# Layer 2's message table as three bf16 parts gathered by TensorE alone, and four lane places in layers 1 and 3

## The reference

```
layer 0: out = [x, mean over src of edge_attr, u]; three times relu(out @ W.T + b), batch norm
layer 1: relu((sum of x[src] by dst / count + x) @ W.T + b)
layer 2: message = [x[src], x[dst]] @ Wmsg[type] + bmsg[type]; agg = mean by dst
         h = [x, agg] @ Wupd + bupd; x + gelu(layer norm(h))
layer 3: sum by dst of dinv[src] * w * dinv[dst] * (x[src] @ W), self loops; relu, batch norm
```

## Time and profile before

| | |
|---|---|
| median of 3 runs | 3917.97 us (3916.83 to 3924.28) |
| profiled execution | 3916.97 us, of which the span of the trace is 3915.2 us |
| busy share of the span | PE 74%, PEld 65%, DVE 60%, ACT 35%, POOL 48% |
| TensorE's granted clock, mean over the span | 0.96 |

### The profile page before, as it was taken

One profiled execution on the slowest core, in us unless ns is written; L12 is line 12 of the kernel. 1 busy time (PEld: TensorE's weight loads), 2 busy tenths in 40 slices (PEclk: granted clock), 3 DMA queues, 4 the chain that ended last, 5 costly groups with the idle time before them and its releaser, 6 DMA issues.

```text
span 3915.2 us, 90566 instructions
## 1 busy us (share of the span) xinstructions
PE 2906.6 (74%) x22101; PEld 2552.1 (65%) x22102; DVE 2356.3 (60%) x6762; ACT 1381.0 (35%) x4186; POOL 1888.7 (48%) x1870
## 2 busy tenths in 40 slices
PE   7455444444459976776998899999879967777996
PEld 6233322222258855776997599999868957776995
DVE  7666666666658885333777544444446774344777
ACT  0111000000024444554664231221246337887534
POOL 4777777777730034776000177777732006774000
PEclk9999999999999988998998999999989978998998
DMA  6444444444458815776884344444467816786883
GB/s 216 147 144 144 145 145 142 142 143 143 141 190 271 271 40 185 267 272 218 288 285 137 131 161 159 155 164 163 122 180 225 272 58 237 267 275 203 276 285 119
DMA packets 430910, 736.77 MB, mean 188 GB/s; under 512 B 71488, under 2 KB 207305, under 8 KB 429820
## 3 DMA queue, kind: packets, MB, share of 16 engines
q1 hardware_dynamic: 336876, 498.35, 41.2%
q0 software_dynamic: 93968, 237.72, 16.6%
HBM read 486.89 MB, written 294.72 MB: 200 GB/s over the span
## 4 chain that ended last, share of the span: by engine, by line
POOL 30%; PE 26%; issue 19%; DMA 13%; DVE 5%; ACT 3%; SPq 2%; DVEq 1%; POOLq 1%; ACTq 0%
POOL slots L704 19%; PE ps L1324 17%; DMA gbuf<-ring_raw,to_blk 7%; POOL gbuf L752 7%; POOL ring_raw L757 3%; DMA ring_raw<-gbuf 3%; DMA ring_raw<-msg_rows,tables 2%; PE ps L1200 2%; PE ps L1367 1%; PE ps L1404 1%; PE ps L1395 1%; ACT ring_raw L942 1%; PE ps L1476 1%; PE ps L1460 1%; DVE stats L1813 1%
## 5 line engine op out<-in xcount | busy, mean ns | idle before, releaser
L752 POOL DMA_INDIRECT gbuf<-ring_raw,to_blk x731 | 752.3, 1029 | 737.4 <-ACT ring_raw L945 383.3
L704 POOL DMA_INDIRECT slots<-ring_raw,idx_edges x782 | 764.3, 977 | 241.6 <-issue 241.6
L1324 PE MATMUL ps<-ring_raw,hot_raw 128*128 128x128 f32 (+2 forms) x6576 | 797.5, 280 | 108.9 <-DVE hot_raw L1749 47.5
L1324 PEld LDWEIGHTS ps<-ring_raw,hot_raw 128*128 128x128 f32 x6576 | 769.6, 194 | 144.4 <-issue 78.9
L1749 DVE TENSOR_TENSOR hot_raw<-dst_lane,lane_ids 128x512 f32<-128x512 f32 x903 | 626.2, 694 | 70.0 <-ACT dst_lane L906 48.8
L1356 PE MATMUL ps<-big,hot_raw 128*128 x5160 | 584.9, 276 | 22.9 <-ACT ring_raw L945 18.5
L1356 PEld LDWEIGHTS ps<-big,hot_raw 128*128 128x128 f32 x5160 | 579.1, 192 | 29.2 <-issue 28.9
L1235 PE MATMUL ps<-big 128*49 128x343 bf16 (+6 forms) x784 | 263.5, 489 | 397.0 <-DVE big L1645 395.7
L945 ACT COPY ring_raw<-ps 128x512 f32<-128x512 f32 x473 | 277.5, 588 | 647.2 <-DMA gbuf<-ring_raw,to_blk 429.0
L1759 DVE TENSOR_TENSOR big<-big,ps 128x128 f32 (+2 forms) x1032 | 293.6, 284 | 314.6 <-PE ps L1324 311.2
L1235 PEld LDWEIGHTS ps<-big 128*49 128x49 bf16 x784 | 113.9, 159 | 539.6 <-DVE big L1645 305.5
(11 more groups left out here) (264 smaller groups left out, 3919.6 us busy)
## 6 DMA issues: line engine op xcount, KB each, us to landing
ring_raw<-gbuf SPq DMA_DIRECT2D x669, 268.0 KB, 3.5
ring_raw<-in_edge_attr SPq DMA_DIRECT2D x111, 448.0 KB, 3.8
zr<-lane_rows SPq DMA_DIRECT2D x129, 384.0 KB
ring_raw<-slots SPq DMA_DIRECT2D x153, 272.0 KB, 3.4
zt<-lane_rows SPq DMA_DIRECT2D x86, 384.0 KB
big<-slots SPq DMA_DIRECT2D x105, 272.0 KB, 3.2
big<-gbuf SPq DMA_DIRECT2D x105, 268.0 KB, 3.8
pays_raw<-key_rows SPq DMA_DIRECT2D x112, 224.0 KB
```

The source lines that it names most:

```text
L704: pool.indirect_dma_start(edges, bass.IndirectOffsetOnAxis(idx_edges[0:n, u, j:j + 1], 0), edge_rows[0:n, u, j, :], None).then_inc(scatter ...
L752: pool.indirect_dma_start(gbuf, bass.IndirectOffsetOnAxis(to_blk[:, t:t + 1], 0), node_rows[:, r, :], None, bounds_check=NBLK - 1, oob_is_ ...
L1324: ins = pe.matmul(bank(r % 3, width), hots[:, r, j * P:(j + 1) * P], rows[:, j, 0:width], start=j == 0, stop=j == BLK - 1)
```

## The change

- The table `msgs` is now three bf16 tables: high, middle and low part, whose sum is the float32 value. ScalarE copies the high part from PSUM, VectorE writes the rest into a ring of five (`rests`), ScalarE copies the middle part from it, GpSimd subtracts to the low part. The bias is added in PSUM by a second matmul with 3 rows, whose bf16 parts GpSimd prepares behind layer 1's scatters (`split_bias`).
- All six tiles of a round are gathered by TensorE, by bf16 one-hots, with 9 matmuls for each edge position. `msg_rows`, its writes, the fetches and the scatters of fetched rows are gone.
- In layers 1 and 3 the lanes of odd rounds have two places of their own (`lane_odd`, in `B`), so a load may run a round ahead. Edge weights are copied (`keep_weights`) to a table of their own, as the parts take the memory of `pays_raw`.

```
-MIX = RING
-WIDE = MIX - 1
-SPAN = {1: RING, 2: WIDE, 3: RING}
-GATHERED = {1: 0, 2: TILES, 3: TILES + RR * WIDE}
+PARTS = 3
+RESTS = 5
+GATHERED = {1: 0, 2: TILES, 3: 2 * TILES}
...
+        msgs = memory[:, 0:PARTS * PART // 2].bitcast(BF16).rearrange("p (s e) -> p s e", s=PARTS)
...
-        hots3 = hot_raw[:, :].rearrange("p (s t n) -> p s t n", s=2, t=TYPES)
+        hots3 = hot_raw[:, TYPED:HOTS].bitcast(BF16).rearrange("p (s t n) -> p s t n", s=2, t=TYPES)
...
+            def load_turn_lanes(layer, h, odd, free=True):
+                i = h * 2 + odd
                 for r in range(0, RING, LANE_SETS):
+                    if free:
+                        sp.wait_ge(src_hots, i * RING + (GATHERED[layer] - 2 * RING + r + LANE_SETS))
...
-                        sp.wait_ge(st["g2"]["r"], NEAR + (i + 1) * STEP)
-                        sp.dma_start(table[:, i * STEP:(i + 1) * STEP, :],
-                                     msgs[:, i * STEP:(i + 1) * STEP, :]).then_inc(msgs_out, 16)
...
-                    for i in range(RR):
-                        for r in range(WIDE):
-                            scatter_block(i, r)
-                            if r == 0 and i > 0:
-                                scatter_fetched(i - 1)
-                            if r == WIDE - 2 and i > 0:
-                                pool.wait_ge(fetched_sent, 16 * i)
-                                pool.sem_inc(issued, 1)
-                            if r >= WIDE - 2:
-                                for k in range(2):
-                                    fetch_messages(i, 2 * (r - WIDE + 2) + k)
-                    scatter_fetched(RR - 1)
+                for i in range(RR):
+                    for r in range(RING):
+                        scatter_block(i, r)
+            def low_parts(n):
+                pool.wait_ge(mid_ready, n + 1)
+                pool.tensor_tensor(part_of(2, n), rests[:, n % RESTS, :], part_of(1, n), ALU.subtract).then_inc(low_ready, 1)
...
             scatter_blocks(1)
+            keep_weights()
+            split_bias()
+            for n in range(GROUPS):
+                low_parts(n)
             scatter_blocks(2)
...
+            def high_part(n):
+                act.wait_ge(st["g2"]["m"], n + 1)
+                act.copy(part_of(0, n), bank(6 + n % 2, TYPES * D)).then_inc(high_ready, 1)
+            def mid_part(n):
+                act.wait_ge(st["g2"]["r"], n + 1)
+                act.copy(part_of(1, n), rests[:, n % RESTS, :]).then_inc(mid_ready, 1)
+            def parts(i, last=False):
+                for n in range(i * STEP, (i + 1) * STEP):
+                    high_part(n)
+                    if n:
+                        mid_part(n - 1)
...
             g2_operands(3)
             g2_copy(3)
             g2_operands(4)
+            parts(3)
             ln_sqrt(2, 2)
             g2_copy(4)
             g2_operands(5)
+            parts(4)
...
+                    for r in range(RING):
+                        pe.wait_ge(src_hots, i * RING + (base + r + 1))
+                        pe.wait_ge(staged, i * RING + (base + r + 1))
                         for j in range(BLK):
                             for t in range(TYPES):
-                                ins = pe.matmul(bank(r)[:, j * P:(j + 1) * P], hots3[:, (odd + r) % 2, t, j * P:(j + 1) * P],
-                                                msgs_flat[:, bass.ds(at[r] + t * D, D)],
-                                                start=t == 0, stop=t == TYPES - 1)
+                                for k in range(PARTS):
+                                    ins = pe.matmul(bank(r)[:, j * P:(j + 1) * P], hots3[:, r % 2, t, j * P:(j + 1) * P],
+                                                    msgs[:, k, bass.ds(at[r] + t * D, D)],
+                                                    start=t == k == 0, stop=t == TYPES - 1 and k == PARTS - 1)
...
+                    n = i * STEP + j
+                    if n > 1:
+                        pe.wait_ge(st["g2"]["r"], n - 1)
+                    pe.matmul(bank(6 + n % 2, TYPES * D), zt2[:, j, :],
                               wcat[:, 0:TYPES, :].rearrange("p k d -> p (k d)"),
-                              start=True, stop=True).then_inc(st["g2"]["m"], 1)
+                              start=True, stop=False, skip_group_check=True)
+                    pe.matmul(bank(6 + n % 2, TYPES * D), part_ones, bias_parts, start=False, stop=True,
+                              skip_group_check=True).then_inc(st["g2"]["m"], 1)
...
-            pe.wait_ge(st["g2"]["r"], NEAR + GROUPS)
+            pe.wait_ge(low_ready, GROUPS)
             gather(2)
...
             def g2_results(i, js=range(STEP)):
                 for j in js:
+                    n = i * STEP + j
+                    dve.wait_ge(high_ready, n + 1)
+                    if n >= RESTS:
+                        dve.wait_ge(low_ready, n - RESTS + 1)
+                    dve.tensor_tensor(rests[:, n % RESTS, :], bank(6 + n % 2, TYPES * D), part_of(0, n),
+                                      ALU.subtract).then_inc(st["g2"]["r"], 1)
```

More of the change, by code:

```diff
@@ L96, in fills_before, with of @@
 def fills_before(stage, r):
-    return sum(EVEN if s in (("g", 0), ("g", 1)) else RR for s in FILLS[:FILLS.index(stage)] if s[0] == "g" or r % LANE_SETS == 0)
+    def of(s):
+        if s[0] == "g":
+            return EVEN if s[1] < 2 else RR
+        if s[1] == 2:
+            return RR if r % LANE_SETS == 0 else 0
+        return (EVEN, ODD, 0)[r % LANE_SETS]
+    return sum(of(s) for s in FILLS[:FILLS.index(stage)])
 LCOLS = 86
@@ L319, in gnn_kernel @@
         to_blk = sb("to_blk", [P, TILES], U32)
-        lanes = sb("lanes", [P, TILES * BLK], BF16)
-        lanes_t = sb("lanes_t", [P, TILES * BLK], BF16)
+        edge_w = sb("edge_w", [P, TILES * BLK])
+        lanes, lanes_t = (edge_w[:, k * TILES * BLK // 2:(k + 1) * TILES * BLK // 2].bitcast(BF16) for k in range(2))
         dst_lane = sb("dst_lane", [P, TILES * BLK])
@@ L350, in gnn_kernel @@
             "p (r n) -> p r n", r=LANE_SETS) for v in (zr, zt)]
+        lane_odd = [B[:, v * (LANE_SETS * BLK * P // 2):(v + 1) * (LANE_SETS * BLK * P // 2)].bitcast(BF16).rearrange(
+            "p (r n) -> p r n", r=LANE_SETS) for v in range(2)]
+        assert 2 * LANE_SETS * BLK * P // 2 <= 4 * COLS
         def bank(b, n=512):
@@ L601, in load_all_lanes @@
             def load_all_lanes(layer):
                 if layer != 2:
-                    load_lanes(layer, 0)
+                    for odd in range(2):
+                        load_turn_lanes(layer, 0, odd, False)
+                    with sp.Fori(1, ODD) as h:
+                        for odd in range(2):
+                            load_turn_lanes(layer, h, odd)
+                    load_turn_lanes(layer, ODD, 0)
+                    return
                 with sp.Fori(1, RR) as i:
-                    load_lanes(layer, i)
+                    load_typed_lanes(i)
@@ L617, in _ @@
+                    load_typed_lanes(0)
                 else:
@@ new lines, in split_bias @@
+            def split_bias():
+                high, mid, low = (bias_work[:, k, 0:TYPES * D // 2].bitcast(BF16) for k in range(3))
+                rest, part, total = (bias_work[:, k, :] for k in range(3, 6))
+                whole = bc[0:PARTS, 0:TYPES, :].rearrange("p k d -> p (k d)")
+                pool.wait_ge(prep_out, 9)
+                steps.mark(pool.memset(part_ones, 1.0))
+                steps.link(pool.tensor_copy(high, whole))
+                steps.link(pool.tensor_tensor(rest, whole, high, ALU.subtract))
+                steps.link(pool.tensor_copy(mid, rest))
+                steps.link(pool.tensor_tensor(low, rest, mid, ALU.subtract))
+                steps.link(pool.tensor_tensor(total, high, ident[0:PARTS, 0:1].broadcast_to([PARTS, TYPES * D]), ALU.mult))
+                for k, v in ((1, mid), (2, low)):
+                    steps.link(pool.tensor_tensor(part, v, ident[0:PARTS, k:k + 1].broadcast_to([PARTS, TYPES * D]), ALU.mult))
+                    steps.link(pool.tensor_tensor(total, total, part, ALU.add))
+                pool.tensor_copy(bias_parts, total).then_inc(lanes_ready, 1)
@@ L1068, in _ @@
             next_copy("f1", 4)
+            parts(0)
             g2_operands(1)
@@ L1071, in _ @@
             next_copy("f1", 5)
+            parts(1)
             ln_sqrt(2, 1)
@@ L1075, in _ @@
             next_copy("f1", 6)
+            parts(2)
             g2_operands(3)
@@ L1774, in source_hots, with typed_hots @@
             def source_hots(layer):
-                base, wide = GATHERED[layer], SPAN[layer]
-                def typed_hots(i, odd):
-                    for r in range(wide):
+                base = GATHERED[layer]
+                def typed_hots(i):
+                    for r in range(RING):
                         if r % LANE_SETS == 0:
```

163 lines of the change are left out of this document (67 added, 96 removed).

## The result

The kernel after takes 3934.0 us (median of 11 runs, 3925.7 to 3944.4), the kernel before 3918.0 (11 runs): ratio 1.0037, 95% interval 1.0026 to 1.0047. The profiled execution has a span of 3930.4 us against 3915.2, +15.2 us. The prediction said slower, by 97 us; it is slower by 16, or 0.4%.

The account below looks back on a forecast made before the run. TensorE's matmuls were taken to pace layer 2's gather, GpSimd's scatters layers 1 and 3. Gather +101, its end -28, table +27, lane places -3 make +97 on 3917 us: 4015 us with 1.0 to the median; range 3880 to 4110.

Parts of the forecast that it names:

- One bf16 matmul at 68.5 ns: Layer 2's gather: 9288 matmuls, each with its own weight load, take 68.5 ns each, 636 us.
- Heads: Starts of layer 2's gather rounds: TensorE idles 1.15 us in each of 43 while offsets are read, 49 us.
- Nine register operations: Behind each round's head in layer 2's gather, address operations slow the first nine matmuls to 0.125 us each, 21 us.
- End of the gather: Between layer 2's gather and the reduction: GpSimd lags by one tile only, leaving 8 us, -28 us.
- Table: Building layer 2's message table in parts: 1.25 us a tile, 114 us for 86.6, +27 us.
- Lane places: Layers 1 and 3: VectorE's waits for lanes vanish but scatters keep their own pitch, -3 us for both.
- The rest hidden: Layer 2's gather: VectorE's one-hots, GpSimd's indirect DMAs and ScalarE's evictions stay covered, 7 us to spare; none becomes the bound.
- Rival B: The change cancels: 57 ns a matmul plus nine register operations, gather 611 us, kernel 3919 us; chance 0.12.

Follow-up runs that it names:

- narrow_even: Kernel after, but each matmul of layer 2's gather moves 98 of 128 message columns; 43 ns a step at the median, gather 585 us.
- rows49: narrow_even with weights and moving operand using 49 of their 128 rows; median step 81 ns, mean 84, at granted clock 0.50.
- block_inner: Kernel after with the gather's four blocks innermost, one address serving four matmuls, some sums incomplete; gather 578.8 us, kernel 3901.4 us, ratio 0.9941 to before.

## Why the prediction was wrong, and where it was right

- **One bf16 matmul at 68.5 ns, 636 us: failed.** It is 56 ns, 520 us: 116 us too much, from which the next two terms, too small by 24, took the gather's error down to 93. The lane turns' 55.5 ns was the right row. The look-ups looked nearer for their own load per matmul, but ran at the lower clock, and I divided their time by matmuls where a triple's goes by columns. The sentence "so I read it as the pace of loads of 128 weight columns" is the error. narrow_even, at both levels of the clock, and rows49 show the law; the doubled durations ahead of 1129 us and the 281 ns of L1245's records show the level.
- **Heads, 49 us:** 55.6. That the read outlasts the queue was right. The size is in part luck: I set a head of 2.0 us against a cover of 1.1. Counted from the read's start, 1.8 us pass to the next round's first matmul, and only eight matmuls are still to come in most rounds (0.45 us).
- **Nine register operations, 21 us:** 25 in the nine thin steps, and 13 behind them of which most is theirs; block_inner took 35 away. The after-effect on the clock was missing. Their count, 2322, was as said.
- **End of the gather, -28 us:** -28.0 (36.6 to 8.6).
- **Table, +27 us:** +34.6, and +31 to +41 over the thirteen traces with this code. The tile's pace, 1.25 us, held at the higher level (1.22), but I took it for all seven steps, and three went at the lower one, at some 2.0 us for my "up to 1.6": the product takes 1.59 us there and the bias product 0.42, for my 1.34 and 0.33.
- **Lane places, -3 us:** 0 or slightly above. Scatters of layer 1 over 342.4 us for 341.2, of layer 3 345.0 for 342.6.
- **The rest hidden:** right; VectorE's one-hots take 0.354 us for the 0.48 allowed.

Rival B had the case: 57 ns with nine operations, gather 611 us, kernel 3919; measured 613 and 3934, half of the difference from the table. Its chance of 0.12 was too low because one misread row held 0.46. That the kernel came out slower, as forecast, is in part luck: of my +97 us the gather had +101, and it gave 8. What makes the kernel slower is the table, to which I had given +27.

## What to carry to other kernels

Price a short matmul by its moving columns and the clock level at which the row ran, and test the level by a like instruction's duration elsewhere, not by the clock column alone where records may be missing. When an engine gets faster, the sequencer's work comes out: issue the matmuls that share an address one behind another, and read offsets where nothing else thins the queue. Before hoping for a shorter chain, see which engine sets a stage's pace at the lower clock.

## What the runs showed that I had not expected

- With 49 of 128 rows in use, TensorE stayed at granted clock 0.50 for 800 us while 98% busy; the same stream with 128 rows (narrow_even) was granted 0.93. No other run here varies the rows.
- A read of six offsets into registers takes 0.8 to 2.2 us (mean 1.44), of 18 up to 5.4 (mean 3.58); what spreads them is open.
- Leaving out 0.42 us of TensorE's work a tile brought the table's stretch to 128 us, below all thirteen traces that have it (142.6 to 153.3), most of it by the clock's level.
